# Mixture of experts on one core: places in pairs of tiles, hidden values formed transposed, weights split per pair, first stage reordered

## The reference, cut to what matters

```python
x = x + tanh(g_xattn) * xattn(layernorm(x), ctx, ctx, lens, lens, W, b)   # 4 x 1024 rows of 256; 77 keys each
x = x + tanh(g_ffn) * ffn(layernorm(x), router_w, w_gate, w_up, w_down)
def ffn(x):                                   # 4096 rows, 8 experts, 2 of them for each row
    top_w, top_i = top_k(softmax(x @ router_w.T), 2);  top_w /= sum(top_w)
    g, u = x @ w_gate[e].T, x @ w_up[e].T     # 256 -> 512
    y = (silu(g) * u) @ w_down[e].T           # 512 -> 256, summed over e with top_w
```

## Time and profile before

| | |
|---|---|
| median of 3 runs | 480.4 us (476.0 to 485.05) |
| the profiled execution | 478.07 us, of which the profile's span is 476.2 us |
| PE busy | 422.5 us, 89% |
| DVE busy | 239.4 us, 50% |
| ACT busy | 192.2 us, 40% |
| POOL busy | 242.1 us, 51% |
| moved by DMA | 49.59 MB |

### The profile page before, as it was taken

The page is one execution under the profiler, slowest core; times in us unless marked ns, Lnnn a source line. Parts: engine busy times, 40 slices in busy tenths (PEclk is TensorE's granted clock), DMA queues, the critical chain, the costliest instruction groups (busy, mean ns, idle before and its releaser), DMA issues.

```text
span 476.2 us, 9017 instructions
## 1 busy us (share of the span) xinstructions
PE 422.5 (89%) x2491; PEld 356.2 (75%) x2492; DVE 239.4 (50%) x748; ACT 192.2 (40%) x480; POOL 242.1 (51%) x310
## 2 busy tenths in 40 slices
PE   7988886630669999999999999999999999999994
PEld 3847665420448888888888888888888898888884
DVE  3115899989935555555555543333333333333331
ACT  2353655302024555454545543343433333343331
POOL 8421676753053555265645555556554645555552
PEclk9595889555589999999999999999999999999999
DMA  6714566688521333833543334243333332423342
GB/s 196 234 46 133 192 214 219 211 284 274 210 70 22 49 67 49 305 55 57 105 124 60 56 56 66 47 67 51 62 55 57 48 63 45 67 45 56 56 66 27
DMA packets 31943, 49.59 MB, mean 104 GB/s; under 512 B 3516, under 2 KB 25489, under 8 KB 31921
## 3 DMA queue, kind: packets, MB, share of 16 engines
q0 software_dynamic: 13152, 18.65, 23.6%
q1 hardware_dynamic: 17511, 29.84, 18.6%
q10 hardware_dynamic: 1258, 0.84, 0.6%
HBM read 31.76 MB, written 17.57 MB: 104 GB/s over the span
## 4 chain that ended last, share of the span: by engine, by line
PE 77%; DVE 11%; DMA 3%; ACT 3%; issue 2%; POOL 2%; POOLq 0%; SPq 0%; ACTq 0%; DVEq 0%
PE GT L1088 19%; PE Y L1115 19%; PE UP L1088 19%; PE HT L1105 6%; PE S L997 4%; PE XT L1079 3%; PE O L1030 3%; DVE at_low L766 2%; DVE at_tile L877 2%; DMA out_rows<-y,idx 2%; ACT ex L559 1%; DVE xg L795 1%; DMA kr<-in_router 1%; DVE st L799 1%; PE O L1016 1%
## 5 line engine op out<-in xcount | busy, mean ns | idle before, releaser
L499 POOL DMA_INDIRECT out_rows<-y,idx x67 | 107.7, 1608 | 141.5 <-ACT y L625 90.2
L1115 PE MATMUL Y<-w_high,hT 128*128 x536 | 107.1, 283 | 0.0
L1088 PE MATMUL GT<-w_high,xtT 128*128 x272 | 102.7, 418 | 0.4 <-issue 0.4
L1088 PE MATMUL UP<-w_high,xtT 128*128 x272 | 102.0, 416 | 0.0
L930 DVE TENSOR_TENSOR hT<-HT,hT 128x512 fp32r<-128x512 f32 x67 | 46.4, 692 | 107.2 <-ACT hT L619 107.2
L491 POOL DMA_INDIRECT xt<-xn_rows,idx x71 | 70.9, 999 | 38.3 <-issue 20.7
L1115 PEld LDWEIGHTS Y<-w_high,hT 128*128 128x128 f32 x536 | 87.7, 190 | 3.0 <-issue 0.3
L625 ACT ACTIVATE y<-Y,xt 128x256 f32<-128x256 f32 x67 | 31.8, 474 | 139.8 <-PE Y L1115 114.3
L1115 PE MATMUL Y<-w_low,hT 128*128 x268 | 67.2, 283 | 0.0
L920 DVE TENSOR_TENSOR xtT<-XT,xtT 128x256 fp32r<-128x256 f32 x69 | 29.3, 425 | 59.6 <-ACT xtT L611 59.5
L1088 PEld LDWEIGHTS GT<-w_high,xtT 128*128 128x128 f32 x272 | 51.4, 189 | 10.3 <-issue 0.9
(11 more groups left out here) (158 smaller groups left out, 531.5 us busy)
## 6 DMA issues: line engine op xcount, KB each, us to landing
raw<-in_weights SPq DMA_DIRECT2D x16, 768.0 KB, 6.6
xn_rows<-pay SPq DMA_DIRECT2D x8, 528.0 KB, 3.2
xTg<-in_xT SPq DMA_DIRECT2D x8, 512.0 KB, 5.9
xg<-in_x SPq DMA_DIRECT2D x8, 512.0 KB, 5.1
out_rows<-xg SPq DMA_DIRECT2D x8, 512.0 KB, 3.3
xt<-xn_rows,idx POOLq DMA_INDIRECT x71, 2.8
out_rows<-y,idx POOLq DMA_INDIRECT x67, 3.8
kr<-in_ctx_rows SPq DMA_DIRECT2D x1, 308.0 KB
```

What stands on the lines that cost most here:

```text
L499: gp.indirect_dma_start(out=out, out_offset=bass.IndirectOffsetOnAxis(ap=idx[:, j:j + 1], axis=0), in_=y[:, j % 2, :], in_offset=None, com ...
L1088: last = mm(bank[:], xtT[:, s % 2, px, c * P:(c + 1) * P], parts[pw][c][:, bass.ds(e * HW + k * HID, HID)], start=(c == 0 and n == 0), sto ...
L1115: last = mm(Y[:, s % 2, 0:D], hT[:, px, c * P:(c + 1) * P], parts[pw][c // (HC // DC)][:, bass.ds(e * HW + DOWN + c % (HC // DC) * D, D)], ...
```

## The change

Stage 2: a turn now handles a pair of tiles, 256 places of one expert (`PT`); each expert is filled up to whole pairs. Gate and up are formed transposed: a block of 128 x 128 weights is stationary, the 256 places move. The hidden values so come out as `down` needs them, and the transposes of the hidden columns are gone. Only the raw weights stay in SBUF. ACT and DVE split the weights of a pair anew in every turn, into one buffer for each half of gate and up and two for down. All raw weights are loaded in stage 1 and right behind the first gathers, a quarter at a time. Each pair has two gathers (four pairs ahead) and two adds; each add still waits for the one before.

Stage 1: the exponentials are no longer scaled by POOL; the scale is put on in the add of the rows (DVE) and in the values. The variance of the new rows comes from ACT's sums of squares, its mean from one more router column. The `at_low` columns are dealt out between other DVE steps. Scores are formed four groups ahead; the values of keys 2 and 3 are formed within the first groups; masks are made by DVE; the loads start without waiting for a memset. `at_tile` is made by four large instructions. `keep_busy` products stand in every turn.

```diff
-TILES = (TOPK * N - NE) // P + NE
+PT = 2 * P
+PAIRS = (TOPK * N - NE) // PT + NE
+TILES = 2 * PAIRS
-XR = 8
-AHEAD = 6
+XR = 4
+AHEAD = XR
...
+            for s in range(AHEAD):
+                sp.wait_ge(tile_loaded[s], 32)
+            for e in range(4, NE):
+                for part in range(PARTS):
+                    sp.wait_ge(raw_loaded, 16 * (PARTS * e + part))
+                    load_weights(e, range(part, part + 1))
...
+            def add(j, t):
+                pool.wait_ge(y_added, 16 * (2 * j + t) + Y_ADDED0)
+                pool.wait_ge(y_ready, 2 * j + t + 1 + Y_READY0)
...
+            for j in range(LEAST):
+                for t in range(2):
+                    add(j, t)
+                    gather(j + AHEAD, t)
...
             for k in range(GROUPS):
+                sum_squares2(k)
...
+                inverse_sqrt(n)
+                if n + 1 < GROUPS:
+                    sum_squares(n + 1, front)
+                if n < GROUPS:
+                    exponentials(n)
                 exp_gap(k)
+                if n + 1 < GROUPS:
+                    sum_squares(n + 1, back)
+                if n < GROUPS:
+                    copy_expT(n)
...
+            def turn(j, s, i, known=None, behind=2):       # ACT
+                    cut_gate_up(j + 1, e1, 0)
+                hid_highs(j, 0)
+                silu(j, 1)
+                if behind > 1:
+                    tile_highs(j + 2, s % 2)
+                hid_highs(j, 1)
+                if behind > 0:
+                    silu(j + 1, 0)
+                    cut_gate_up(j + 1, e1, 1)
+                    cut_down(j + 1, e1, (s + 1) % 2)
+                weigh(j, s, e)
...
+            for c in range(0, UNITS, CHUNK):
+                tt(out=at_tile[:, c:c + CHUNK], in0=iota_t[:].unsqueeze(1).to_broadcast([P, CHUNK, TILES]),
+                   in1=col[:, c:c + CHUNK].unsqueeze(2).to_broadcast([P, CHUNK, TILES]),
+                   op=ALU.is_equal).then_inc(tile_hot, 1)
...
+            def turn(j, s, i, e=None, behind=2):           # DVE
+                gate_up(j, 0)
+                    cut_gate_up(j + 1, e1, 0)
+                hid_lows(j, 0)
+                gate_up(j, 1)
+                    tile_lows(j + 2, s % 2)
+                hid_lows(j, 1)
+                    cut_gate_up(j + 1, e1, 1)
+                    cut_down(j + 1, e1, (s + 1) % 2)
...
+            def first_layer(bank, b, q, w):                # PE, gate (w=0) and up (w=1), half q
+                for h in range(2):
+                    for c in range(DC):
+                        for n, (px, pw) in enumerate(HI_LO):
+                            last = mm(bank[:, h * PT:(h + 1) * PT], gu[:, pw, q, c, w, h * P:(h + 1) * P], xtT[:, b, px, c],
...
+            def turn(j, s, i, none=None, behind=2):        # PE
+                gate(j, b, 1)
+                up(j, b, 1)
+                    transpose_pair(j + 2, (s + 2) % XR, i + (s + 2) // XR)
+                    gate(j + 1, 1 - b, 0)
+                down(j, b)
+                    up(j + 1, 1 - b, 0)
```

More of the change, by code:

```diff
@@ L790, in _ @@
                 dve.wait_ge(attn_ready, k + 1)
-                at = slot_of(k)
-                added = []
-                for t in range(0, G, 2):
-                    pair = xg[:, at + t:at + t + 2]
-                    added.append(mark(tt(out=pair, in0=O[:, t:t + 2, 0:D], in1=pair, op=ALU.add)))
-                tt(out=lg1[:], in0=O[:, :, D:OW], in1=sr[:, q], op=ALU.add).then_inc(attn_used, 1)
-                for t in range(G):
-                    after(added[t // 2])
-                    last = v.bn_stats(st2[:, t], rows(k, t))
@@ new lines, in _ @@
+                add_rows(0).then_inc(rows_added, 1)
+                after(scaled)
+                summed = mark(tt(out=lg1[:], in0=lg0[:], in1=sr[:, q], op=ALU.add))
+                add_rows(1).then_inc(rows_added, 1)
+                after(summed)
+                ts(negmean2[:, q], lg1[:, :, NE], -1.0 / D, None, ALU.mult).then_inc(negmean2_ready, 1)
+                add_rows(2).then_inc(rows_added, 1)
+                add_rows(3).then_inc(rows_added, 1)
+                behind = k - 2
+                at_lows(behind, range(0, 2))
@@ L811, in _ @@
-                after(moments)
-                ts(ve[:, q, G:2 * G], mv[:, :, 1], EPS, float(D), ALU.add, ALU.mult).then_inc(var_ready, 1)
-                if more:
-                    router_part(n)
+                    router_part(n)
+                if k > 0:
+                    own = own_ranks(k - 1)
+                    at_lows(behind, range(2, 3))
+                    ranked = unit_ranks(k - 1, own)
+                    at_lows(behind, range(3, 4))
+                    masked = low_bits(k - 1, ranked)
+                    at_lows(behind, range(4, 5))
+                    low_places(k - 1, masked)
@@ L870, in _ @@
             after(begun)
-            after(mark(tt(out=starts[:], in0=oh[:].rearrange("p g c t e -> p (g c t) e"),
-                          in1=start[:].unsqueeze(1).to_broadcast([P, UNITS, NE]), op=ALU.mult)))
-            after(mark(v.tensor_reduce(first[:], starts[:], axis=AX.X, op=ALU.add)))
-            after(high_bits)
-            after(mark(tt(out=col[:], in0=first[:], in1=high[:], op=ALU.add)))
-            for u in range(UNITS):
-                last = ts(at_tile[:, u], iota_t[:], col[:, u:u + 1], None, ALU.is_equal)
-                if u % CU == CU - 1:
-                    last.then_inc(tile_hot, 1)
@@ L932, in _ @@
[L932 to L935 removed]
+            after(mark(tt(out=past[:], in0=J[:].unsqueeze(2).to_broadcast([1, PAIRS, NE]),
+                          in1=cum[0:1, :].unsqueeze(1).to_broadcast([1, PAIRS, NE]), op=ALU.is_ge)))
+            after(mark(v.tensor_reduce(tex[:], past[:], axis=AX.X, op=ALU.add)))
+            ts(pairs_used[:], cum[0:1, NE - 1:NE], 0.5, None, ALU.mult)
@@ L956, in _ @@
[L956 to L964 removed]
+            cut_down(0, e, 0)
@@ L1156, in _ @@
-            last_tiles(pe, tile)
+                if k + 4 < GROUPS:
+                    scores(k + 4)
+                    if k >= 2:
+                        keep_busy(4)
+                elif k + 1 < GROUPS:
+                    keep_busy(13)
+            keep_busy(22)
+            pe.wait_ge(picks_ready, GROUPS)
+            counts = L[:, COUNTS:COUNTS + NE]
+            mm(counts, ones[:], carry[:, GROUPS - 1], start=True, stop=False)
+            for t in range(G):
+                last = mm(counts, ones[:], picks[:, GROUPS - 1, t], start=False, stop=(t == G - 1))
@@ new lines, in _ @@
+            last.then_inc(counts_ready, 1)
+            ranks(GROUPS - 1)
+            keep_busy(18)
+            for u in range(UNITS):
+                if u % CHUNK == 0:
+                    pe.wait_ge(tile_hot, u // CHUNK + 1)
+                if u % CU == 0:
+                    pe.wait_ge(low_ready, u // CU + 1)
+                last = mm(L[:, LIST:LIST + TILES], at_low[:, u], at_tile[:, u], start=(u == 0), stop=(u == UNITS - 1))
+            last.then_inc(list_ready, 1)
+            keep_busy(22)
```

934 lines of the change are left out of this document (455 added, 479 removed).

## The result

| | before | after |
|---|---|---|
| median of 6 runs each | 481.6 us (476.0 to 485.05) | **437.5 us** (435.52 to 438.52) |
| the profiled execution, and its span | 478.07, 476.2 us | 438.52, 436.7 us |
| PE, DVE, ACT, POOL busy | 89, 50, 40, 51% | 95, 72, 65, 58% |

Executions more than 1.5% above the fastest of their kernel are left out of every comparison of this document, which leaves four of the six before, with a median of 479.6 us. The ratio is 0.912, with a 95% interval of 0.906 to 0.918: faster by 42 us. The forecast was 456, in a range of 440 to 474; the time lies 2.5 us under its lower end. What came closest is the first rival, PE setting the pace (440).

A forecast was written before the change was run, and what follows sets the result against it. PE was taken to bound stage 2, DVE and ACT round trips the groups; after the change, the adds stage 2. 478.07 - 22.8 (stage 1) + 3.1 (start of stage 2) - 2.5 (adds) gave 456 us, range 440 to 474.

The forecast's parts named there:

- the first rival: Stage 2: PE sets the pace after all, at 9.03 us per pair, 440 us in all; chance 0.14.
- What bounds the kernel now: Kernel before: PE bounds stage 2, busy 321.24 of 322.40 us; DVE and round trips over ACT pace the eight groups.
- PE's turn, ACT and DVE: Stage 2, per pair: PE 9.03 us, ACT 7.4, DVE 7.1; 34 pairs, 68 adds, PE not stalled.
- The adds, then, set the pace: 67 x 4.62: Stage 2: adds follow each other at 4.62 us, 313.3 us from first add's start to last landing.
- Adds land sooner: Stage 2: one way for PE to set the pace, landings below 3.8 us; the least seen was 3.6.
- No price for cuts and loads: Stage 2: other way for PE to set the pace, the adds paying neither 6.3 us for cuts nor 4 for loads.
- The port and the loads: Stage 2: adds wait for running DVE cuts, 6.3 us, and are slowed by loads of later experts' weights, 4 us.
- 0.23 for about 16 adds and 0.05 for the rest: Stage 2: us each add waits for what is left of a DVE instruction, 6.3 us in all.
- The slow rival: Stage 2: each add meets a cut at its start and pays 0.8 us, 54 for 6.3, 504 us; chance 0.07.
- Stage 1: Up to `idx`: first rows at 26.5 us, groups 59, lists 22; ends at 107.5 us for 130.3, -22.8.
- -3, my estimate, bounds 0 and -5: Before the first rows: keys start 1.2 us earlier, masks off POOL, one batch of keys first, 3 us less.
- The start of stage 2: From `idx` to the first add: 21.5 us for 18.4, +3.1, bounds +1 and +6.

## Why the prediction was wrong

**What bounds the kernel now**: right. PE in stage 2, DVE and round trips in stage 1.

**PE's turn, ACT and DVE**: right. 9.06 us for 9.03; cuts of 1.04 us (ACT) and 1.22 (DVE) for 1.12 and 1.21; 34 pairs, 68 adds; PE waits for no cut.

**"The adds, then, set the pace: 67 x 4.62"**: this is the step that failed. 4.62 us is 3.8 us of landing and 0.8 us to the next start, and the 0.8 belongs to the order of the waits in the kernel before. The change turns the order, and I read that in the diff and took it for nothing. With it the adds can be 4.10 us apart, 4.3 to 4.4 behind a cut, and PE with 4.53 per tile sets the pace: 308.8 us from the first add to the last landing, for 323.6. The kernel with the old order shows that the rest of this argument was sound: there the adds do set the pace, at 463.9 us. The first rival, 440 us, named the right bound, but neither of its reasons holds. "Adds land sooner": they do not, the median is 3.9 us for 3.8. "No price for cuts and loads": without these prices 67 x 4.62 + 3.8 is still 313.3. It got 0.14.

**The port and the loads**: mechanism right, sizes off. The formula for one add (what is left of the cut, less 0.12 us) gives the issues of the kernel with the old order and of the changed kernel within 0.04 us, but for one, which started 0.02 us behind the start of a DVE instruction and paid nothing. The mean of 0.23 us per add, worked out from it, was right: 0.24 where the adds set the pace. What failed is the step from there, "0.23 for about 16 adds and 0.05 for the rest", 6.3 us: it is 16 us over all 68. The guess that adds would start as ACT begins a cut, when DVE has none, was the wrong phase, since 37 of the 68 met one. The slow rival's 0.8 us per add did not come. In the changed kernel these prices lie under PE's time. The loads were 6 us for 4. By the Trainium skill, SBUF — State Buffer (SBUF: two separate sides), a DVE instruction with two SBUF inputs and a GpSimd one that reads SBUF shut each other out of a shared pair of ports, and the one that starts first keeps it for the whole instruction. The traces agree where DVE's instruction is already running (the issue is 1.05 us longer at worst). Where it starts during the issue they agree only in part. The issue isn't held up; DVE's cut isn't either, which by the Trainium skill it would be. (The adds read their row numbers `idx` from SBUF.) In the kernel with the old order a cut begins 0.01 us behind an add; the add takes its 1.59 us, and the cut 1.25 for 1.22:

```profile
319.14 1.59 POOL L503 DMA_INDIRECT out_rows<-y,idx  x1 [1.46 <-DMA out_rows<-y,idx]
```

```profile
319.15 1.25 DVE L973 TENSOR_TENSOR dn<-raw,dn 128x1024 fp32r<-128x1024 f32 x1
```

**Stage 1**: 102.1 us for 107.5. The groups (58.1 for 59) and the lists (21.5 for 22) were right in size. The first rows came at 22.5 for 26.5, 4 us off in a sum of five terms, of which "-3, my estimate, bounds 0 and -5" had no row at all; which term it was, no run here separates. That PE is the bound of a group and the unread products fill it was not right: groups without them, at the full clock, were no shorter, and at half the clock all of them together took 3 us more. The start of stage 2, +5.4 for +3.1, was the clock at 1.2 GHz during its first products (2.3 us).

**Sum**, by the same terms: 438.5 = 455.9 - 14.8 (adds) - 5.4 (stage 1) + 2.4 (start) + 0.4 (the rest).

## What to carry to other kernels

When a queue becomes the bound on paper, take apart its interval: the part that is a wait's price belongs to the code of the kernel before, and a diff that turns two waits changes it. Of two waits ahead of an indirect transfer on GpSimd, write last the one that has usually long been met; and see what stands behind that transfer in the same queue. Where a bound has only a few per cent of slack under the next, size that one too: here 26 us hung on the order of two lines.

## What the runs showed of the hardware

- A wait written directly ahead of an indirect transfer on GpSimd, if it is the one that ends last, starts it 0.79 us behind a landing; with another, already met wait between them it is 0.27. For ACT's result it is 0.80 and 0.28. All in both kernels, for most adds; every seventh or eighth starts 0.1 to 0.25 us later still. Why it is so, no run here shows.
- An indirect transfer that starts t us into a running DVE instruction with two SBUF inputs takes the rest of that instruction, less 0.12 us, more: 0.14 for 0.26 us left, 0.49 for 0.61, 1.05 for 1.17. A DVE instruction that starts while the issue runs, or up to 0.03 us ahead of it, costs it nothing; nor does one with an input in PSUM (the add at 303.35 us of the changed kernel, with 0.47 us left of a product `hid`, took 1.59).
- The granted clock was 0.50 from 49.9 to 53.3 us in one execution (more unread products at the start of stage 2) and 1.00 there in another (the changed kernel), with the same instructions up to there. A difference of 2 us in stage 1 between two executions is no result.
